# Attention with three probability buffers and a reordered turn; linear attention written out over sixteen blocks

## The chip, the cores and the metric

The kernel runs on one core of one Trainium2 chip. The metric is the device time of one execution in microseconds; of a kernel the median of its runs is taken. Before the change it is 1459.32 us, the median of three runs between 1455.14 and 1463.46 us.

The engines that appear below are PE (TensorE, matrix multiplications; its weight loads are listed as PEld), ACT (ScalarE), DVE (VectorE), POOL (GpSimd) and SP, which issues DMAs.

## The reference

The reference is a small transformer-like network over 16 images of 113 tokens (36 patches and 77 text tokens) with 256 features. Four layers follow each other, each an attention-like block and a feed-forward block with residuals. Only two blocks matter here, cut to their core:

```python
# third layer, its attention part: no softmax
theta_x = einsum('bnf,lf->bnl', x, W_theta)      # 64 latent features
phi_x   = einsum('bnf,lf->bnl', x, W_phi)
fun_g_x = einsum('bnf,of->bno', x, W_g)
att     = einsum('bnl,bml->bnm', theta_x, phi_x) / 16
out     = einsum('bnm,bmo->bno', att, fun_g_x)

# fourth layer, its attention part: 16 heads of 16 features
Wqk     = einsum('hij,hkj->hik', tril, tril)
scores  = einsum('bshe,bthe->bhst', x_h @ Wqk, x_h) / 4
attn    = softmax(scores)
out     = (attn @ (x @ Wv.T + bv)) @ Wo.T + bo
```

All is in 32-bit floats, and x is the layer-normalised state.

## The kernel before

The state `core.h` stays on chip as 113 rows by 16 blocks (images) by 256 features. Before each block a stage normalises it and turns it to features by tokens, split into two 16-bit halves, `xt_hi` and `xt_lo`. A product of two 32-bit matrices is then three 16-bit matmuls, made by `mm3` (lines 459 to 463): high by high, high by low, low by high. A result that feeds another product is split in the same way: ACT rounds it to the high half, DVE or POOL subtracts to get the low half. Each stage is one program block, in which every engine runs its own written-out or looped order, and engines wait for one another on counting semaphores. `need(eng, sem, n)` is such a wait that is left out for counts of zero or less.

**Linear attention** (`stage_linear_attention`, line 2775). Since no softmax stands between, phi and g are first multiplied to a 64 by 256 matrix per image. Four operations of PE: `theta` for a group of four images (2 x 3 matmuls of 452 columns), `project` for one image (6 matmuls of 320 columns: phi and g side by side), `collect` (phi times g, 3 matmuls of 256 columns), `spread` (theta times that matrix, 3 matmuls). In the profile their results are la_pth, la_ppg, la_pm and la_po, in this order. ACT and DVE split after `theta`, `project` and `collect`; DVE adds the result of `spread` to the state. A hardware loop runs over the four groups; `theta` has one buffer, so a pass starts with `theta`, and the order of a pass is project(0), then for each j: project(j+1), collect(j), spread(j-1), at last spread(3). The other buffers are double.

**Attention** (`stage_attention`, line 3079). Written out over 17 turns; turn j works on image j, ahead on j+1 and j+2, behind on j-1. Per image the 16 heads go in four groups g of four. `project_u` makes the head-wise factors, `take_q` (ACT) and `split_u` (DVE) split them, `first_pass` makes scores for the row maxima, DVE takes the maxima, repeats them (`repeat_peaks`), PE transposes them (`turn_peaks`), ACT and DVE split them (`take_qm`, `split_peaks`), and `second_pass` makes the scores again with the maximum subtracted. Then per group: `exponential` (ACT, line 3309) into a 32-bit buffer `prob`, `round_prob` (ACT, line 3315) into `prob_hi`, POOL's subtraction into `prob_lo` (line 3146), and `weigh_v` on PE (line 3228, 20 small matmuls), which also makes the sums of the rows. `project_v` makes the values, and `normalize`, `take_o`, `split_o`, `project_out`, `add` finish the image. `keep_warm` issues four matmuls whose result nobody reads. `prob` has two buffers: exponential g waits for the low half of g-2.

Beside this, each turn prepares two pieces of the weights of the last stage (`CutWeights`): ACT casts both (line 1515), scales one in place (line 1520), POOL subtracts for the scaled one (line 1530, behind `prob_lo` of its turn), DVE for the other (line 1524). SP loads the pieces.

The order of ACT in a turn before the change: exponential 0 and 1, take_v, round_prob 0 and 1, take_q(j+2), exponential 2 and 3, take_o(j-1), round_prob 2 and 3, take_qm(j+1), two casts, one scaling. PE's: second_pass(0), first_pass(j+1, 0), keep_warm, second_pass(2), project_u(j+2), first_pass(j+1, 2), keep_warm, weigh_v 0 and 1, project_v(j+1), turn_peaks(j+1), project_out(j-1), weigh_v 2 and 3.

Of the kernel before, what the change touches and what calls it, by code (L numbers as in the profile page):

```python
# [6 lines left out]
F16 = mybir.dt.float16  # L7
I32 = mybir.dt.int32
U32 = mybir.dt.uint32
ALU = mybir.AluOpType  # L10
# [3 lines left out]
NB = 16  # L14
# [2760 lines left out]
def stage_linear_attention(nc, core, d, w):  # L2775
# [3 lines left out]
    with Stage(nc, "la") as st:  # L2779
        wt_hi, wt_lo, wg_hi, wg_lo = w.wt_hi, w.wt_lo, w.wg_hi, w.wg_lo  # L2780
        th_hi, th_lo = (st.sb(n, [Z, GT], F16) for n in ("th_hi", "th_lo"))
        two = range(2)
        pg_hi, pg_lo = ([st.sb(f"{n}{p}", [L, W2], F16) for p in two] for n in ("pg_hi", "pg_lo"))
        m_hi, m_lo = ([st.sb(f"{n}{p}", [Z, D], F16) for p in two] for n in ("m_hi", "m_lo"))
        pth = st.ps("pth", [Z, 512])
        ppg, pm, po = ([st.ps(f"{n}{p}", [s, 512]) for p in two] for n, s in (("ppg", L), ("pm", Z), ("po", L)))
        th_ready, th_high, th_split = st.sem("th_ready"), st.sem("th_high"), st.sem("th_split")
        g_ready, g_high, g_split, m_ready, m_high, m_split, o_ready, o_free = (
            [st.sem(f"{n}{p}") for p in two] for n in (
                "g_ready", "g_high", "g_split", "m_ready", "m_high", "m_split", "o_ready", "o_free"))  # L2790
        with nc.Block() as block:
            @block.tensor
            def _(pe):
                with pe.Fori(0, NG) as q:
                    cols = bass.ds(q * GT, GT)
                    pe.wait_ge(th_split, q)
                    for k in range(KC):
                        last = mm3(pe, pth[:, 0:GT], wt_hi[:, k, :], wt_lo[:, k, :], core.xt_hi[:, k, cols],
                                   core.xt_lo[:, k, cols], k == 0, k == KC - 1)
                    last.then_inc(th_ready, 1)  # L2800

                    def project(j):
                        p = j % 2
                        tok = bass.ds(q * GT + j * L, L)

                        pe.wait_ge(g_split[p], q * 2 + j // 2)
                        for k in range(KC):
                            last = mm3(pe, ppg[p][:, 0:W2], core.xt_hi[:, k, tok], core.xt_lo[:, k, tok],
                                       wg_hi[:, k, :], wg_lo[:, k, :], k == 0, k == KC - 1)
                        last.then_inc(g_ready[p], 1)  # L2810

                    def collect(j):
                        p, before = j % 2, q * 2 + j // 2
                        pe.wait_ge(g_split[p], before + 1)
                        pe.wait_ge(m_split[p], before)
                        mm3(pe, pm[p][:, 0:D], pg_hi[p][:, 0:Z], pg_lo[p][:, 0:Z], pg_hi[p][:, Z:W2],
                            pg_lo[p][:, Z:W2], True, True).then_inc(m_ready[p], 1)

                    def spread(j):
                        p, before = j % 2, q * 2 + j // 2  # L2820
                        pe.wait_ge(th_split, q + 1)
                        pe.wait_ge(m_split[p], before + 1)
                        pe.wait_ge(o_free[p], before)
                        tok = slice(j * L, (j + 1) * L)
                        mm3(pe, po[p][:, 0:D], th_hi[:, tok], th_lo[:, tok], m_hi[p][:], m_lo[p][:], True,
                            True).then_inc(o_ready[p], 1)

                    project(0)
                    for j in range(GB):
                        if j + 1 < GB:  # L2830
                            project(j + 1)
                        collect(j)
                        if j:
                            spread(j - 1)
                    spread(GB - 1)

            @block.scalar
            def _(act):
                with act.Fori(0, NG) as q:
                    act.wait_ge(th_ready, q + 1)  # L2840

                    for p in two:
                        act.wait_ge(o_ready[p], q * 2)
                    act.activation(th_hi[:], pth[:, 0:GT], ACT.Copy, scale=1.0 / WS).then_inc(th_high, 1)
                    for j in range(GB):
                        p, before = j % 2, q * 2 + j // 2
                        act.wait_ge(g_ready[p], before + 1)
                        act.wait_ge(m_ready[p], before)
                        act.activation(pg_hi[p][:], ppg[p][:, 0:W2], ACT.Copy, scale=1.0 / WS).then_inc(g_high[p], 1)
                        act.wait_ge(m_ready[p], before + 1)  # L2850
                        act.wait_ge(o_ready[p], before)
                        act.activation(m_hi[p][:], pm[p][:, 0:D], ACT.Copy, scale=1.0 / 16).then_inc(m_high[p], 1)

            @block.vector
            def _(dve):
                def add(q, j):
                    p = j % 2
                    dve.wait_ge(o_ready[p], q * 2 + (j // 2 + 1))
                    b = bass.ds(q * GB + j, 1)
# [3 lines left out]
                with dve.Fori(0, NG) as q:  # L2863
# [3 lines left out]
                    for j in range(GB):  # L2867
# [7 lines left out]
                        if j:  # L2875
                            add(q, j - 1)
# [755 lines left out]
```

## Time and profile before

| | us |
|---|---|
| median of three runs | 1459.32 |
| the profiled execution | 1472.0 |
| its span | 1470.3 |
| PE busy | 1047.1 (71%) |
| DVE busy | 1028.9 (70%) |
| ACT busy | 751.0 (51%) |
| POOL busy | 519.4 (35%) |

The profile is of one execution, not of the median run. Times in rows count from the start of its span. The program is a sequence of stages with different limits, so that the shares above say little about any one; the rows below are of the two stages at hand, at 865 to 918 us and 1062 to 1238 us.

### The profile page before, as it was taken

The page shows a single profiled execution, that of the slowest core. Times are in us where ns is not written, and L with a number is a line of the kernel's source. Part 1 is how long each engine was busy: PE and PEld are TensorE (multiplying, and loading weights), DVE is VectorE, ACT ScalarE, POOL GpSimd, SP SyncE. Part 2 cuts the span into 40 slices and gives each one's busy share as a digit, 9 for nine tenths or more (in the row PEclk, how much of TensorE's full clock was granted, in tenths as well). Part 3 has the DMA queues.
Part 4 walks back from the last instruction along what each step waited for, and adds up shares of the span by engine and source line. Part 5 has one row for each costly group of instructions (what it writes and reads, how often), then busy time and mean ns, then how long its engine had stood idle before and what let it go on. Part 6 is the DMA issues. An engine that isn't in the chain of part 4 may idle for free. (4 is left out here: it accounts for less than half of the span.)

```text
span 1470.3 us, 28385 instructions
## 1 busy us (share of the span) xinstructions
PE 1047.1 (71%) x9099; PEld 705.2 (48%) x9099; DVE 1028.9 (70%) x2229; ACT 751.0 (51%) x1493; POOL 519.4 (35%) x620
## 2 busy tenths in 40 slices
PE   3558877753699986766658867266589995389991
PEld 2322322232356553554446744144466663388880
DVE  5779999987256445567967654788758887646552
ACT  5557777742476653125437632244358885244440
POOL 0249888850444427501011100000136665122204
PEclk9669999975799998788978978589669997589996
DMA  5001111000465644202000000000013331112214
GB/s 227 15 22 37 43 43 43 29 26 26 129 165 149 165 137 135 70 6 86 1 0 1 1 1 0 0 0 0 19 69 107 114 117 57 47 51 66 66 48 122
DMA packets 50687, 89.84 MB, mean 61 GB/s; under 512 B 8555, under 2 KB 34867, under 8 KB 49715
## 3 DMA queue, kind: packets, MB, share of 16 engines
q1 hardware_dynamic: 43360, 67.20, 14.3%
q0 software_dynamic: 6912, 18.88, 4.8%
q10 hardware_dynamic: 288, 2.10, 0.5%
q8 instruction: 76, 1.25, 0.3%
q14 instruction: 51, 0.42, 0.1%
HBM read 72.11 MB, written 16.04 MB: 60 GB/s over the span
## 5 line engine op out<-in xcount | busy, mean ns | idle before, releaser
L1133 POOL TENSOR_TENSOR scan_ch<-scan_hs,scan_ct 128x452 f32<-128x452 f32 x128 | 143.6, 1143 | 40.7 <-DVE scan_hs L1247 36.9
L1158 PE MATMUL scan_py<-scan_ch,ident 128*128 128x452 f32 x256 | 131.0, 601 | 37.7 <-POOL scan_ch L1133 28.0
L1247 DVE TENSOR_TENSOR_SCAN scan_hs<-scan_abar,scan_bx 128x452 f32<-128x452 f32 x128 | 133.2, 1084 | 1.2 <-DVE scan_bx L1239 0.6
L2224 DVE TENSOR_SCALAR m3x_a<-m3x_ph,m3x_b 128x128 f32<-128x128 f32 x184 | 49.7, 343 | 68.4 <-ACT m3x_ah L2202 66.2
L1158 PEld LDWEIGHTS scan_py<-scan_ch,ident 128*128 128x128 f32 x256 | 40.6, 193 | 107.0 <-POOL scan_ch L1133 100.2
L1207 ACT ACTIVATE scan_abar<-ssm_dt,ssm_a 128x448 f32<-128x448 f32 x128 | 79.8, 634 | 13.2 <-DVE scan_hs L1247 12.7
L2202 ACT ACTIVATE m3x_ah<-m3x_ph,m3x_b 128x128 f16<-128x128 f32 x184 | 50.1, 383 | 65.0 <-PE m3x_ph L463 60.9
L3146 POOL TENSOR_TENSOR mha_prob_lo<-mha_prob,mha_prob_hi 113x452 f16<-113x452 f32 x64 | 65.8, 1051 | 38.2 <-ACT mha_prob_hi L3315 38.2
L461 PE MATMUL m3x_ph<-m3x_xb,m_w_hi 128*128 128x128 f16 x368 | 74.3, 223 | 2.6 <-DVE m3x_al L2235 2.2
L462 PE MATMUL m3x_ph<-m3x_xb,m_w_hi 128*128 128x128 f16 x368 | 74.4, 224 | 0.0
L463 PE MATMUL m3x_ph<-m3x_xb,m_w_lo 128*128 128x128 f16 x368 | 74.2, 223 | 0.0
L1239 DVE TENSOR_TENSOR scan_bx<-scan_pb,ssm_dx 128x452 f32<-128x452 f32 x128 | 73.2, 615 | 0.4 <-PE scan_pb L1145 0.4
L2020 DVE TENSOR_TENSOR m0x_a<-m0x_ph,m0x_gate 128x256 f32<-128x256 f32 x57 | 24.2, 424 | 68.1 <-ACT m0x_gate L1980 67.8
L669 POOL TENSOR_SCALAR mhaf_xr<-h,rstd,mhaf_shift 113x256 f32<-113x256 f32 x5 | 2.9, 592 | 193.9 <-DVE mhaf_shift L734 193.9
L2297 POOL DMA_INDIRECT shared_got<-m_out,m_slot x48 | 50.3, 1048 | 48.5 <-issue 34.9
L1889 POOL DMA_INDIRECT m0x_xg<-m_rows,m0x_idx x57 | 57.4, 1007 | 15.7 <-POOL m0x_idx L1887 15.4
L1202 ACT ACTIVATE scan_ct<-scan_pc 128x452 f32<-128x452 f32 x64 | 34.5, 539 | 39.1 <-POOL scan_ch L1133 25.0
L461 PE MATMUL m3x_py<-m_w_hi,m3x_ah 128*128 x184 | 50.1, 272 | 1.0 <-DVE m3x_yo L2242 0.8
L463 PE MATMUL m3x_py<-m_w_hi,m3x_al 128*128 x184 | 50.1, 272 | 0.0
L462 PE MATMUL m3x_py<-m_w_lo,m3x_ah 128*128 x184 | 50.1, 272 | 0.0
L1530 POOL TENSOR_TENSOR m_w_lo<-mha_wbuf,m_w_hi 128x1024 f16<-128x1024 f32 x16 | 34.1, 2130 | 32.9 <-ACT mha_wbuf L1520 32.9
L1921 PE MATMUL m0x_ph<-m_w_hi,m0x_xb 128*128 x114 | 44.3, 389 | 1.1 <-ACT m0x_xb L1973 1.1
(697 smaller groups left out, 3808.2 us busy)
## 6 DMA issues: line engine op xcount, KB each, us to landing
mha_wbuf<-m3w SPq DMA_DIRECT2D x32, 512.0 KB, 3.3
scan_piece<-m0w SPq DMA_DIRECT2D x30, 256.0 KB, 2.7
m0x_b<-m0b SPq DMA_DIRECT2D x57, 128.0 KB
m_out<-m0x_yo SPq DMA_DIRECT2D x57, 128.0 KB
tok_wbuf<-m0w SPq DMA_DIRECT2D x5, 768.0 KB, 9.4
m3x_b<-m3b SPq DMA_DIRECT2D x23, 128.0 KB, 3.1
m_out<-m3x_yo SPq DMA_DIRECT2D x23, 128.0 KB
m_rows<-m0r_parts SPq DMA_DIRECT2D x4, 448.0 KB
```

The source lines that it names most:

```text
L461: pe.matmul(out, w_hi, x_hi, start=start, stop=False)
L462: pe.matmul(out, w_hi, x_lo, start=False, stop=False)
L463: return pe.matmul(out, w_lo, x_hi, start=False, stop=stop)
L1133: pool.tensor_tensor(ch[r][:], hs[r][:], ct[n % 2][:], ALU.mult).then_inc(weighed, 1)
L1158: pe.matmul(py[c][:, 0:GT], core.ident[:], ch[u % R][:], start=n == 0, stop=n == NS - 1).then_inc(summed, 1)
L1207: act.activation(abar[c][:, 0:GT].rearrange("p (b t) -> p b t", t=L)[:, :, 1:L], ssm.dt[:, c, cols].rearrange("p (b t) -> p b t", t=L)[:, ...
L1239: dve.tensor_tensor(bx[u % R][:], pb[n % 2][:, 0:GT], ssm.dx[:, c, cols], ALU.mult).then_inc(drive, 1)
L1247: dve.tensor_tensor_scan(hs[u % R][:], abar[c][:, 0:GT], bx[u % R][:], 0.0, ALU.mult, ALU.add).then_inc(scanned, 1)
L1889: pool.indirect_dma_start(xg[p][:], None, m.rows[:, :], bass.IndirectOffsetOnAxis(ap=idx[p][:, 0:1], axis=0)).then_inc(gathered[p], 16)
L2202: ins = act.activation(a_hi[r][:, f, :], ph[p][:, f, :], ACT.Relu, bias=b1[p][:, 0, f:f + 1])
L2297: pool.indirect_dma_start(self.got[j][k][:], None, m.out[:, :], bass.IndirectOffsetOnAxis(ap=m.slot[:, b, k:k + 1], axis=0)).then_inc(self ...
L3146: pool.tensor_tensor(prob_lo[g][:], prob[g % 2][:], prob_hi[g][:], ALU.subtract).then_inc(p_low, 1)
```

## The change

Linear attention: the hardware loop over groups is replaced by an order written out over all 16 blocks. `theta` gets two buffers on chip and in PSUM. PE's order is project(0), theta(0), project(1), and then for each block b: collect(b); theta of the next group, if b is the second block of its group; spread(b-1); project(b+2). ACT and DVE follow the same order. The semaphores that were one for each of two buffers become one counter each.

Attention: `prob` has three buffers, so exponential g waits for the low half of g-3. Exponential 2 stands ahead of take_q(j+2). weigh_v(3) of a turn is issued in the next turn, behind second_pass(0) and first_pass(0). The reciprocal of the sums is written into `o` and multiplied in place; the buffer `rec` goes, and the wait for `split_o` of the block before stands ahead of the reciprocal.

```diff
+                project(0)
+                theta(0)
+                project(1)
+                for b in range(NB):
+                    collect(b)
+                    if b % GB == 1 and b // GB + 1 < NG:
+                        theta(b // GB + 1)
+                    if b:
+                        spread(b - 1)
+                    if b + 2 < NB:
+                        project(b + 2)
+                spread(NB - 1)
...
+                high_gate(0)
+                high_theta(0)
+                high_gate(1)
+                for b in range(NB):
+                    high_memory(b)
+                    if b % GB == 1 and b // GB + 1 < NG:
+                        high_theta(b // GB + 1)
+                    if b + 2 < NB:
+                        high_gate(b + 2)
...
+                for b in range(NB):
+                    low_memory(b)
+                    if b % GB == 1 and b // GB + 1 < NG:
+                        low_theta(b // GB + 1)
+                    if b:
+                        add(b - 1)
+                    if b + 2 < NB:
+                        low_gate(b + 2)
+                add(NB - 1)
...
-        prob = [st.sb(f"prob{r}", [L, HG, L]) for r in two]
+        prob = [st.sb(f"prob{r}", [L, HG, L]) for r in range(3)]
...
-                        pool.tensor_tensor(prob_lo[g][:], prob[g % 2][:], prob_hi[g][:],
+                        pool.tensor_tensor(prob_lo[g][:], prob[(j * 4 + g) % 3][:], prob_hi[g][:],
...
                     if ahead1:
                         first_pass(j + 1, 1 - p, 0)
+                    if behind:
+                        weigh_v(j - 1, 1 - p, 3)
                     if now:
                         keep_warm(4)
                         second_pass(j, p, 2)
...
                     if now:
                         weigh_v(j, p, 2)
-                        weigh_v(j, p, 3)
...
-                    need(act, p_low, j * 4 + (g - 1))
-                    act.activation(prob[g % 2][:], heads(s2[g % 2]), ACT.Exp, scale=0.25).then_inc(exped, 1)
+                    need(act, p_low, j * 4 + (g - 2))
+                    act.activation(prob[(j * 4 + g) % 3][:], heads(s2[g % 2]), ACT.Exp, scale=0.25).then_inc(exped, 1)
...
+                    if now:
+                        exponential(j, 2)
                     if ahead2:
                         take_q(j + 2)
                     if now:
-                        exponential(j, 2)
                         exponential(j, 3)
...
-                    need(dve, o_made, j)
-                    dve.reciprocal(rec[:], pacc[:, KC * L:2 * KC * L]).then_inc(rec_ready, 1)
+
+                    need(dve, ol_ready, j)
+                    dve.reciprocal(o[:], pacc[:, KC * L:2 * KC * L]).then_inc(rec_ready, 1)
                     dve.wait_ge(rec_ready, j + 1)
-
-                    need(dve, ol_ready, j)
-                    dve.tensor_tensor(o[:], pacc[:, 0:KC * L], rec[:], ALU.mult).then_inc(o_made, 1)
+                    dve.tensor_tensor(o[:], pacc[:, 0:KC * L], o[:], ALU.mult).then_inc(o_made, 1)
```

## Rows read from the trace of the kernel before

**Rows 1.** Table by stretches: busy time by engine (instructions), granted clock, DMA.

```profile
core 0: us, PE busy (x) PEld busy (x) DVE busy (x) ACT busy (x) POOL busy (x), PEclk, DMA share, GB/s
865.60:918.20 52.60, 42.35 (x216) 25.61 (x216) 21.65 (x52) 13.82 (x36) 0.00 (x0) 0.86 0.00 0
870.00:879.00 9.00, 6.38 (x41) 3.76 (x39) 4.34 (x11) 2.65 (x8) 0.00 (x0) 1.00 0.01 2
879.00:883.00 4.00, 4.00 (x15) 2.52 (x16) 1.05 (x2) 0.86 (x2) 0.00 (x0) 0.58 0.00 0
...
1108.50:1222.20 113.70, 105.02 (x2358) 75.93 (x2356) 96.67 (x167) 99.39 (x179) 74.29 (x60) 1.00 0.35 114
```

**Rows 2.** Timeline of PE, linear attention: start, duration, instruction, idle time before.

```profile
899.59 0.30 PE L461 MATMUL la_pm<-la_pg_hi 113*64 113x256 f16 x1 [0.36 <-DVE la_pg_lo L2870]
900.03 0.32 PE L461 MATMUL la_po<-la_m_hi,la_th_hi 64*113 64x256 f16 x1
900.50 0.34 PE L461 MATMUL la_ppg<-la_wg_hi,xt_hi 128*113 128x320 f16 x1
...
903.91 0.30 PE L461 MATMUL la_pm<-la_pg_hi 113*64 113x256 f16 x1 [1.19 <-DVE la_pg_lo L2870]
...
905.97 0.37 PE L461 MATMUL la_pth<-xt_hi,la_wt_hi 128*64 x1
...
907.23 0.34 PE L461 MATMUL la_ppg<-la_wg_hi,xt_hi 128*113 128x320 f16 x1
...
908.09 0.30 PE L461 MATMUL la_ppg<-la_wg_hi,xt_hi 128*113 128x320 f16 x1
...
909.30 0.30 PE L461 MATMUL la_pm<-la_pg_hi 113*64 113x256 f16 x1 [0.24 <-DVE la_pg_lo L2870]
```

**Rows 3.** Timeline of DVE, linear attention.

```profile
900.55 0.42 DVE L2873 SCALAR_TENSOR_TENSOR la_m_lo<-la_pm,la_m_hi 64x256 f16<-64x256 f32 x1 [1.02 <-ACT la_m_hi L2852]
```

**Rows 4.** Timeline of ACT, one attention turn.

```profile
1146.39 1.06 ACT L1520 ACTIVATE mha_wbuf<-mha_wbuf 128x1024 f32<-128x1024 f32 x1
...
1150.05 0.64 ACT L3290 ACTIVATE mha_q<-mha_pu,mha_to_q 128x452 f16<-128x452 f32 x1 [0.52 <-PE mha_pu L463]
...
1151.77 0.55 ACT L3309 ACTIVATE mha_prob<-mha_s 113x452 f32<-113x452 f32 x1 [0.46 <-POOL mha_prob_lo L3146]
...
1153.59 0.36 ACT L3303 ACTIVATE mha_qm<-mha_pt,mha_to_qm 128x113 f16<-128x113 f32 x1
...
1155.87 1.06 ACT L1520 ACTIVATE mha_wbuf<-mha_wbuf 128x1024 f32<-128x1024 f32 x1
```

**Rows 5.** Timeline of POOL, the same turn.

```profile
1147.53 2.13 POOL L1530 TENSOR_TENSOR m_w_lo<-mha_wbuf,m_w_hi 128x1024 f16<-128x1024 f32 x1 [1.82 <-ACT mha_wbuf L1520]
1149.62 2.05 POOL L3146 TENSOR_TENSOR mha_prob_lo<-mha_prob,mha_prob_hi 113x452 f16<-113x452 f32 x2
```

**Rows 6.** Timeline of PE, the same turn.

```profile
1148.47 0.26 PE L3203 MATMUL mha_s<-mha_same 32*113 32x113 f16 x2 [0.32 <-ACT mha_prob L3309]
...
1151.72 0.23 PE L3228 MATMUL mha_pacc<-mha_prob_hi,mha_v_hi 113*32 113x113 f16 x4
...
1153.24 0.32 PE L3190 MATMUL mha_pt<-ident,mha_peaks 113*128 113x113 f32 x1
...
1155.24 0.23 PE L3228 MATMUL mha_pacc<-mha_prob_hi,mha_v_hi 113*32 113x113 f16 x4 [0.32 <-POOL mha_prob_lo L3146]
```

**Rows 7.** Timelines of ACT and DVE, the first turns and the last.

```profile
1087.59 1.06 ACT L1520 ACTIVATE mha_wbuf<-mha_wbuf 128x1024 f32<-128x1024 f32 x1
1099.02 1.06 ACT L1520 ACTIVATE mha_wbuf<-mha_wbuf 128x1024 f32<-128x1024 f32 x1
1222.21 1.06 ACT L1520 ACTIVATE mha_wbuf<-mha_wbuf 128x1024 f32<-128x1024 f32 x1
1226.56 0.55 ACT L3309 ACTIVATE mha_prob<-mha_s 113x452 f32<-113x452 f32 x1 [1.22 <-POOL mha_prob_lo L3146]
...
1231.99 1.56 DVE L3395 RECIPROCAL mha_rec<-mha_pacc 128x226 f32<-128x226 f32 x1
```

More of the change, by code:

```diff
@@ L2793, in _, with theta @@
             def _(pe):
-                with pe.Fori(0, NG) as q:
-                    cols = bass.ds(q * GT, GT)
-                    pe.wait_ge(th_split, q)
+                def theta(q):
+                    p, cols = q % 2, slice(q * GT, (q + 1) * GT)
+                    need(pe, th_split, q - 1)
                     for k in range(KC):
-                        last = mm3(pe, pth[:, 0:GT], wt_hi[:, k, :], wt_lo[:, k, :], core.xt_hi[:, k, cols],
+                        last = mm3(pe, pth[p][:, 0:GT], wt_hi[:, k, :], wt_lo[:, k, :], core.xt_hi[:, k, cols],
@@ L2812, in collect @@
[L2812 to L2835, printed above, removed]
+                def project(b):
+                    p, tok = b % 2, slice(b * L, (b + 1) * L)
+                    need(pe, g_split, b - 1)
+                    for k in range(KC):
+                        last = mm3(pe, ppg[p][:, 0:W2], core.xt_hi[:, k, tok], core.xt_lo[:, k, tok],
+                                   wg_hi[:, k, :], wg_lo[:, k, :], k == 0, k == KC - 1)
+                    last.then_inc(g_ready, 1)
@@ new lines, in collect, with spread @@
+                def collect(b):
+                    p = b % 2
+                    pe.wait_ge(g_split, b + 1)
+                    need(pe, m_split, b - 1)
+                    mm3(pe, pm[p][:, 0:D], pg_hi[p][:, 0:Z], pg_lo[p][:, 0:Z], pg_hi[p][:, Z:W2],
+                        pg_lo[p][:, Z:W2], True, True).then_inc(m_ready, 1)
+                def spread(b):
+                    p, g = b % 2, b // GB % 2
+                    pe.wait_ge(th_split, b // GB + 1)
+                    pe.wait_ge(m_split, b + 1)
+                    need(pe, o_free, b - 1)
+                    tok = slice(b % GB * L, (b % GB + 1) * L)
+                    mm3(pe, po[p][:, 0:D], th_hi[g][:, tok], th_lo[g][:, tok], m_hi[p][:], m_lo[p][:], True,
+                        True).then_inc(o_ready, 1)
@@ L2840, in _ @@
                     act.wait_ge(th_ready, q + 1)
[L2842 to L2852, printed above, removed]
+                    need(act, o_ready, (q - 1) * GB)
@@ L2863, in _, with low_theta, low_gate @@
[L2863 removed]
+                def low_theta(q):
+                    p = q % 2
                     dve.wait_ge(th_high, q + 1)
[L2865 removed]
+                    dve.scalar_tensor_tensor(th_lo[p][:], pth[p][:, 0:GT], 1.0 / WS, th_hi[p][:], ALU.mult,
                                              ALU.subtract).then_inc(th_split, 1)
[L2867 to L2877 removed]
+                def low_gate(b):
+                    p = b % 2
+                    dve.wait_ge(g_high, b + 1)
+                    dve.scalar_tensor_tensor(pg_lo[p][:], ppg[p][:, 0:W2], 1.0 / WS, pg_hi[p][:], ALU.mult,
+                                             ALU.subtract).then_inc(g_split, 1)
```

65 lines of the change are left out of this document (32 added, 33 removed).

## The prediction

> **What bounds the kernel now.** I read the page first: no engine is busy for more than 71% of the span, so an average decides nothing, and the two stages that the change touches have to be read by themselves. Next came the table by stretches. Linear attention runs from 865.6 to 918.2 us with the matmul engine (PE) busy 42.35 of 52.6 us at a mean granted clock of 0.86; the clock is 1.00 (2.4 GHz) at 870 to 879 us, but 0.58 at 879 to 883, where for most of the time the lower level, 1.2 GHz, was granted [rows 1]. The attention turns run at 1.00 [rows 1]. The timelines by engine followed.
>
> Linear attention has two kinds of lost PE time. Within a group of four blocks PE waits on each round trip through ScalarE (ACT) and VectorE (DVE): a `collect` waits up to 1.19 us for `pg_lo` [rows 2]. At the seams between loop passes PE drains and restarts with `theta`; 879 to 883 is such a seam.
>
> Attention is paced differently. One turn (one image) lasts 9.48 us: the scaling of the weight buffer, ACT's last work in a turn, starts at 1146.39 and again at 1155.87 [rows 4]. Inside the turn ACT idles 0.52 us before `take_q` (for PE) and 0.46 us before the fourth exponential (for GpSimd, POOL) [rows 4]. These two are what the change removes from ACT. But whether they set the turn must be read from a closed loop of dependencies, and there is one whose links all touch: ACT scales the buffer (1146.39), POOL subtracts `m_w_lo` from 1147.53 for 2.13 us, then, back to back, `prob_lo` 0 and 1 from 1149.62 for 2.05 us, until 1151.67 [rows 5]; PE's `weigh_v(1)` starts at 1151.72; after it and `project_v`, the transpose of the peaks starts at 1153.24 and lasts 0.32, until 1153.56 [rows 6]; ACT's `take_qm` starts at 1153.59, and behind it, after the two casts of the weights, the next scaling at 1155.87 [rows 4]. The steps are 1.14 + 2.09 + 2.10 + 1.52 + 0.35 + 2.28 = 9.48 us: the whole turn, with no slack in it.
>
> **The change, part by part.**
>
> *Three probability buffers.* The fourth exponential then waits for `prob_lo` 0 (half way through the pair, about 1150.65) in place of `prob_lo` 1 (1151.67): 0.46 us of ACT per turn is gone. *Third exponential ahead of `take_q`.* It runs in the 0.52 us in which ACT waited for PE's `pu`: its scores come from the second pass that PE started at 1148.47 [rows 6], before the projection that `take_q` waits for. Together 0.98 us of ACT per turn. What is late next? `take_qm`. It stands behind `round_prob` 3, which now ends about 1 us earlier, but its input still comes at 1153.56, by the loop above, and no link of that loop is touched: same subtraction, same `prob_lo` 0 and 1, same PE order from `weigh_v(1)` to the transpose, same casts. So ACT trades two short waits for one of about 1 us before `take_qm`, and the turn stays 9.48. Value for the 13 turns from 1099.02 to 1222.21 (their scalings start 14 times in that stretch, 9.48 apart on the mean: 123.19 / 13 [rows 7]): 0 us. The bounds: no loss below 0, and the most it could give is B below.
>
> *`weigh_v(3)` moved behind the next turn's first two passes.* Before, it waited 0.32 us for `prob_lo` 3 and started at 1155.24 [rows 6], at the end of the turn. Its 20 matmuls of 113 columns, four side by side, take some 0.3 to 0.4 us (estimate: at 0.86 us for six matmuls of 320 columns [rows 2], five steps of 113 make 0.25, and the change of operation is on top). Now PE goes straight to the second pass, which fills the scores some 0.7 us earlier; ACT cannot use them earlier, being still at its scaling until about 1156.9. The 20 matmuls then lie ahead of four warming matmuls and of the second pass of groups 2 and 3, which waited 0.32 us for ACT's exponential, until 1148.47 [rows 6]. They bring no more work to PE before that point than was taken away ahead of the first passes, so it is reached no later than before. Queued behind it on PE is everything from those warming matmuls on; on DVE `normalize` waits for it, but stands behind two maxima and `split_v`; on ACT `take_v` waits for it, about 1 us later. Cost: 0 in the turns at full clock. In turn 1, which lasts 11.43 us [rows 7] and which I read as paced by PE at half clock, I allow 0.1 us.
>
> *Reciprocal written into `o`.* It waits for `split_o` of the block before, which DVE itself issued earlier in its order: 0, and no instruction is added.
>
> *The last turn and the tail.* Turn 15 has no `take_q` and no `take_qm`, so the loop is open there. Its third exponential waited 1.22 us for `prob_lo` 0 and started at 1226.56 [rows 7], the fourth one subtraction (1.03) later. Now only the fourth waits for `prob_lo` 0, and starts where the third did: 1.0 us earlier. Everything behind it (`take_o`, two roundings, casts, DVE's `low`, and the last `normalize`, at 1231.99 [rows 7]) moves up by some 1.0. Attention in sum: 0 - 1.0 + 0.1 = -0.9 us.
>
> *Linear attention written out.* The work is the same (16 blocks, 4 `theta`); what changes is that the order runs across groups with double-buffered `theta` and `project` two blocks ahead. At full clock, start to start: collect to spread 0.44, spread to project 0.47, a whole project 0.86 (907.23 to 908.09), theta 1.26 (905.97 to 907.23) [rows 2]. Sum on PE: 16 x (0.44 + 0.47 + 0.86) + 4 x 1.26 = 28.3 + 5.0 = 33.3 us.
> Do the round trips fit in? `spread(b)` needs `m_lo`: collect at 899.59, `m_lo` from 900.55 for 0.42 [rows 2, 3], 1.4 us; the new order gives it a block and a collect, 1.77 + 0.44 = 2.2. `collect` needs `pg_lo`: 907.23 to 909.30 is 2.07 us [rows 2]; the new order gives 0.86 + 1.77 = 2.6. DVE has three operations a block like the one of rows 3 (0.42 us for 256 columns; some 1.3 us, an estimate), ACT two, against 1.77 us. So PE runs without a gap in the middle, and I take it that it keeps full clock there. To the 33.3 come: the start at half clock (1.9 us: I take it for as long as at the seam of rows 1, 3.8 us, and half of it lost), the last three blocks, where no project lies between (2.07 - 1.77 = 0.3, and 1.4 - 0.44 - 0.47 = 0.5), and the last result's way through DVE after PE's own time (0.8, about one latency and one 0.42): 36.8 us in place of 52.6. Gain 15.7 us.
> Bounds: if a block went on taking 2.16 us, half of the way from the collect at 899.59 to the one at 903.91 [rows 2], 16 x 2.16 + 5.0 + 3.5 = 43 us, a gain of 9.5; if the start cost nothing extra and the tail were hidden, 34.5 us, a gain of 18.
>
> A rule that speaks against this: the Trainium skill, "TensorE: Matmul & The Clock Gate", section "A second HAM failure mode: psum-queue depth-cycling", says that a kernel which cycles through PSUM banks in each iteration idles PE in tiny gaps often enough that its clock swings between both levels. The new order does cycle through eight banks. By that rule the stage would keep its drops; in this trace the drops stand at the seams, where PE waits on the round trip before and after, and the attention turns, which also go round several banks, hold 1.00 [rows 1]. I give it a share of rival C.
>
> **Sum.** 15.7 + 0.9 = 16.6 us. The profiled execution took 1472.0 us (span 1470.3 and 1.7 around it), so 1455.4 by its own time. It was 0.87% slower than the median of the runs, 1459.32; scaled, 1455.4 x 1459.32 / 1472.0 = 1443 us.
>
> **The rivals.**
> A (forecast): as above, 1443.
> B: the turn follows ACT's own work. Then each of the 13 turns shrinks from 9.48 to what PE needs, 9.48 less its waits of 0.32 and 0.32 [rows 6] and some 0.1 at `weigh_v(1)`: 8.74, 9.6 us more: 1433. (ACT alone would allow 8.50.) For it: ACT is the engine with the most work in a turn and both its gaps go. Against: the closed loop of rows 4 to 6, which would have to be wrong in a link; I looked for slack in each and found at most 0.1 us. The Trainium skill, "Perfetto Trace Analysis", section "Optimization Strategy", reads a gap that repeats on the busy engine as too few buffers. By it the third buffer alone would give 0.46 us in each of 13 turns, 6 us; the 0.46 gap does repeat [rows 4], and I hold that it is not the one that paces.
> C: linear attention keeps part of its loss, by the round trip (2.16 us a block) or by half-clock stretches as at 879 to 883 [rows 1]. Gain 9.5 in place of 15.7: 1449. For it: no such dense order of these operations is in the trace. Against: the slack of 0.8 and 0.5 us in the two round trips above.
> D (other side): PE's clock in attention. The move joins two short waits of PE into one of some 0.7 us a turn, and if the granted clock fell for it, turns would be paced by PE at half clock, as I read turn 1: from the scaling at 1087.59 to that at 1099.02 [rows 7], 11.43 us, 1.95 more than 9.48. Nine such turns of the 13 eat the whole gain; with all 13 it is 25.4 us, 1443 + 25 = 1468, slower than before. Against: PE's idle time per turn does not grow, and the clock held 1.00 with waits of this size spread over the turn.
>
> **How the numbers follow.** A 0.69, B 0.09, C 0.16, D 0.06. About 0.5% (7.3 us) is what a measurement of this kernel can tell from no change, since its three runs spread over 8 us. Faster by more than that means below 1452.0: A, B and nearly all of C, 0.90; within it: the rest of C and the mild cases of D, 0.06; slower: 0.04. The predicted time is A's, 1443. The range is 1435 to 1451: A with its bounds (gain 9.5 to 18 in linear attention) and the spread of the runs, C's 1449 inside, half of B's way inside, B's end and D left out.
>
> **What would show it.** Right: linear attention in 36 to 38 us, PE busy throughout at clock 1.0 but for the first 4 us; attention turns still 9.48 us from scaling to scaling, ACT's waits for `pu` and `prob_lo` gone, a wait of about 1 us before `take_qm` in their place; the end of attention some 16.6 us earlier. Wrong: turns of 9.0 us or less (B), a granted clock below 0.9 in the middle of linear attention or collects that wait for `pg_lo` (C), turns over 10 us (D). A shift of a few us in untouched stages, with no instruction changed, would be the clock falling at other places.

## The result, and the profile after

| | us |
|---|---|
| changed kernel, median of 14 runs | 1451.48 (1448.04 to 1454.98) |
| kernel before, median of 14 runs beside them | 1460.74 (1455.14 to 1463.54) |
| ratio | 0.9939, 95% interval [0.9926, 0.9951] |
| predicted | 1443, range 1435 to 1451 |
| profiled execution of the changed kernel, its span | 1449.0, 1447.3 |

Faster by 9 us where 16 were forecast. The two profiled executions are 23 us apart, of which 13 lie ahead of linear attention (865.6 against 852.9 us at its start), where no instruction differs; they belong to no part of the change. So each stage is compared by its own length.

*Linear attention* did what was forecast. The old order starts with `theta`, the new one with project(0), 1.75 us ahead of its first `theta`. From PE's first instruction of the stage (852.86) to the end of DVE's last addition (890.56) it lasts 37.7 us, against 52.5 in the profile before and 51.8 in a second profile of the old order (run e2 below). The table by stretches, which begins at the first `theta`, answers to [rows 1]:

```profile
core 0: us, PE busy (x) PEld busy (x) DVE busy (x) ACT busy (x) POOL busy (x), PEclk, DMA share, GB/s
854.60:890.60 36.00, 34.87 (x211) 22.01 (x210) 20.96 (x52) 15.19 (x36) 0.00 (x0) 0.97 0.00 1
858.00:888.00 30.00, 29.98 (x190) 19.55 (x189) 18.26 (x47) 13.83 (x33) 0.00 (x0) 1.00 0.00 1
```

PE is busy 29.98 of 30 us at full clock; no seam is left. The timeline of PE answers to [rows 2]: the start, from collect to collect 1.86 us, and a stall of the tail.

```profile
852.86 0.49 PE L461 MATMUL la_ppg<-la_wg_hi,xt_hi 128*113 128x320 f16 x1 [1.91 <-PEq L663]
...
862.37 0.30 PE L461 MATMUL la_pm<-la_pg_hi 113*64 113x256 f16 x1
...
864.23 0.30 PE L461 MATMUL la_pm<-la_pg_hi 113*64 113x256 f16 x1
...
889.60 0.29 PE L461 MATMUL la_po<-la_m_hi,la_th_hi 64*113 64x256 f16 x1 [0.50 <-issue]
```

*Attention* did not. It should have become 0.9 us shorter and became 4.8 us longer: from the first write of `pu` to the last of `pvo`, 174.3 us before and 179.1 after. By turns 1 to 15 (scaling to scaling): 11.43, thirteen of 9.46 to 9.48 and 9.05 before; 11.54, eight of 9.47 or 9.48, then 9.54, 9.65, 9.66, **14.99**, 9.47 and 8.32 after. A normal turn on ACT answers to [rows 4]:

```profile
1141.14 1.04 ACT L3349 ACTIVATE mha_prob_hi<-mha_prob 113x452 f16<-113x452 f32 x2
1143.25 0.36 ACT L3337 ACTIVATE mha_qm<-mha_pt,mha_to_qm 128x113 f16<-128x113 f32 x1 [1.07 <-PE mha_pt L3223]
...
1145.53 1.06 ACT L1520 ACTIVATE mha_wbuf<-mha_wbuf 128x1024 f32<-128x1024 f32 x1
```

Both short waits are gone and one of 1.07 us ahead of `take_qm` stands in their place. But the roundings `prob_hi` 2 and 3, directly ahead of it, moved too. In [rows 4] they must have ended by 1153.59, when `take_qm` started without a wait; now they end 1.07 us ahead of it. POOL's `prob_lo` 2 and 3, which follow them, move with them onto other work of DVE. DVE's and POOL's timelines of two turns, a normal one and the first slow one (`x2` is two instructions in one line):

```profile
1141.72 0.23 DVE L3418 TENSOR_SCALAR mha_peaks<-mha_peak 113x128 f32<-113x128 f32 x1
1141.86 1.24 DVE L3438 TENSOR_TENSOR mha_ot_lo<-mha_o,mha_ot_hi 128x226 f16<-128x226 f32 x1
...
1151.30 1.09 DVE L3418 TENSOR_SCALAR mha_peaks<-mha_peak 113x128 f32<-113x128 f32 x1
1152.31 1.25 DVE L3438 TENSOR_TENSOR mha_ot_lo<-mha_o,mha_ot_hi 128x226 f16<-128x226 f32 x1
```

```profile
1141.79 2.21 POOL L3179 TENSOR_TENSOR mha_prob_lo<-mha_prob,mha_prob_hi 113x452 f16<-113x452 f32 x2 [0.46 <-ACT mha_prob_hi L3349]
...
1151.26 2.04 POOL L3179 TENSOR_TENSOR mha_prob_lo<-mha_prob,mha_prob_hi 113x452 f16<-113x452 f32 x2 [0.46 <-ACT mha_prob_hi L3349]
```

In the kernel before, POOL's pair began at 1153.14 in the turn of [rows 4], behind both operations of DVE, and the groups of instructions of DVE give their means over 15 and 14 turns:

```profile
L3404 DVE TENSOR_TENSOR mha_ot_lo<-mha_o,mha_ot_hi 128x226 f16<-128x226 f32 x15 | 5.9, 395 | 5.8 <-ACT mha_ot_hi L3320 5.8
L3383 DVE TENSOR_SCALAR mha_peaks<-mha_peak 113x128 f32<-113x128 f32 x14 | 3.2, 227 | 0.5
```

Now `split_o` (the line of `ot_lo`) lasts 1.24 us in every turn, and `repeat_peaks` 0.23 where it starts 0.07 us ahead of POOL's pair, but 1.09 where it starts 0.04 behind. That is on the loop, since the transpose waits for it. What puts it behind is a slip of 0.09 us in the tenth turn. DVE's reciprocal starts 0.34 us behind the start of `v_lo` in turn 9 and 0.43 in turn 10, and the maxima and `repeat_peaks` follow it:

```profile
1138.28 0.42 DVE L3405 SCALAR_TENSOR_TENSOR mha_v_lo<-mha_pvo,mha_v_hi 113x256 f16<-113x256 f32 x1
1138.62 1.56 DVE L3431 RECIPROCAL mha_o<-mha_pacc 128x226 f32<-128x226 f32 x1
...
1147.76 0.42 DVE L3405 SCALAR_TENSOR_TENSOR mha_v_lo<-mha_pvo,mha_v_hi 113x256 f16<-113x256 f32 x1
1148.19 1.57 DVE L3431 RECIPROCAL mha_o<-mha_pacc 128x226 f32<-128x226 f32 x1
```

With both stretched DVE is full (19.00 of 19.20 us), PE waits 0.85 us for `ot_lo`, the turn lasts 9.65, and after three turns with a stretched `repeat_peaks` PE's clock falls to the lower level, which makes one turn of 14.99:

```profile
1145.50:1164.70 19.20, 16.91 (x370) 11.94 (x366) 19.00 (x28) 16.44 (x30) 12.47 (x10) 1.00 0.35 113
1164.70:1174.40 9.70, 8.85 (x209) 6.38 (x197) 9.63 (x15) 8.24 (x16) 6.29 (x5) 1.00 0.33 110
1174.40:1189.40 15.00, 15.00 (x223) 10.99 (x216) 9.88 (x16) 8.45 (x16) 6.32 (x5) 0.54 0.22 72
```

```profile
1153.61 0.32 PE L461 MATMUL mha_pvo<-mha_wo_hi,mha_ot_hi 128*113 128x256 f16 x1 [0.85 <-DVE mha_ot_lo L3438]
...
1163.26 0.32 PE L461 MATMUL mha_pvo<-mha_wo_hi,mha_ot_hi 128*113 128x256 f16 x1 [0.85 <-DVE mha_ot_lo L3438]
...
1172.91 0.32 PE L461 MATMUL mha_pvo<-mha_wo_hi,mha_ot_hi 128*113 128x256 f16 x1 [0.84 <-DVE mha_ot_lo L3438]
```

### The profile page after: what moved, and what is told of

Same layout as the page of the kernel before. It is cut to its first block and busy times, and to the rows that moved or that the text cites. A ratio compares the mean times of both kernels' runs of the same rounds, so it can differ in the third digit from the quotient of the medians.

```text
span 1447.3 us, 28190 instructions
## 1 busy us (share of the span) xinstructions
PE 1039.5 (72%) x9099; PEld 702.8 (49%) x9099; DVE 1040.7 (72%) x2229; ACT 750.4 (52%) x1493; POOL 521.0 (36%) x620
## 5 line engine op out<-in xcount | busy, mean ns | idle before, releaser
L1889 POOL DMA_INDIRECT m0x_xg<-m_rows,m0x_idx x57 | 57.6, 1010 | 15.7 <-POOL m0x_idx L1887 15.7
```

The lines of the kernel that those rows point to most:

```text
L1889: pool.indirect_dma_start(xg[p][:], None, m.rows[:, :], bass.IndirectOffsetOnAxis(ap=idx[p][:, 0:1], axis=0)).then_inc(gathered[p], 16)
```

## Experiments

All in one table; "attention" and the turns are of each kernel's one profile, medians and ratios of four to six timed executions (twelve for e2) beside the kernel before (1459 to 1461 us). "Full turns" are turns 2 to 14, "others" their lengths: where one value stands, nearly all have it. "clock" marks turns that the clock's fall made long.

| run | median us | ratio [95%] | attention | turn 1 | others |
|---|---|---|---|---|---|
| e1 linear part only | 1443.67 | 0.9878 [0.9859, 0.9896] | 171.9 | 9.47 | 9.47 |
| e2 attention part only | 1461.68 | 1.0012 [0.9995, 1.0028] | 174.5 | 13.05 | 9.48 |
| e3 roundings held | 1446.98 | 0.9899 [0.9881, 0.9918] | 175.4 | 13.03 | 9.48, one 9.55 |
| e4 weigh_v(3) back | 1447.46 | 0.9907 [0.9888, 0.9925] | 176.3 | 9.48 | 9.48, 9.56, clock 13.96 |
| e5 peaks first | 1439.65 | 0.9869 [0.9846, 0.9892] | 168.2 | 8.59 | 8.85 or 9.74 |
| e7 fill | 1443.95 | 0.9901 [0.9881, 0.9921] | 174.8 | 13.01 | 9.48, 9.55, 9.58 |
| e10 weigh_v(3) moved only | 1445.70 | 0.9912 [0.9893, 0.9931] | 175.7 | 13.05 | 9.47 |
| e11 held, weigh_v(3) back | 1443.23 | 0.9902 [0.988, 0.9923] | 172.0 | 9.48 | 9.49, one 9.55 |
| e13 values early | 1443.34 | 0.9867 [0.9829, 0.9906] | 171.8 | 11.65 | clock 13.53, 12.6; 8.66 |
| e14 low behind peaks | 1445.15 | 0.9900 [0.9872, 0.9928] | 175.7 | 12.57 | 9.47 |
| e15 e14 and e5 | 1430.45 | 0.9805 [0.9775, 0.9835] | 161.2 | 8.58 | 8.85 |
| e16 e15, weigh_v(3) back | 1435.09 | 0.9834 [0.9804, 0.9863] | 164.5 | 8.58 | 9.10 |
| e17 e10 and warm end | 1443.02 | 0.9889 [0.9867, 0.9911] | 172.7 | 9.48 | 9.48 |
| e18 e14 and warm end | 1440.48 | 0.9874 [0.9851, 0.9897] | 171.4 | 9.47 | 9.48 |
| e19 changed again | 1451.72 | one execution | 181.9 | 13.05 | 9.48, 9.55, clock 14.01, 10.75 |

**The halves of the change.** e1 is the kernel before with the new `stage_linear_attention`, e2 the changed kernel with the old one.

> Attention as before, linear attention as changed. T1 (linear attention gives some 15.7 us, and the changed attention takes about 5 back, because POOL's prob_lo 2 and 3 now run beside DVE's repeat_peaks and split_o and stretch them from 0.23 to 1.1 and from 0.40 to 1.24 us, so that DVE paces some turns and PE's clock falls): 15 to 17 us under the kernel before, attention from its first take_q to its last add 174 us as before. T3 (linear attention gives only some 9 us in the median, and what the profile of the changed kernel shows in attention is chance): 8 to 10 us under it.

> Linear attention as before, attention as changed. T1: 3 to 7 us slower than the kernel before, split_o at 1.24 us in most turns, some turns of 9.65 us or more. T2 (what costs is the new place of weigh_v(3) on PE, not DVE): the same time. T3: 1 us faster, at most equal.

The linear half alone is worth 1.22%, 17.8 us by the ratio, all of the change's gain and more; the attention half alone gives nothing (0.9995 to 1.0028), and on top of the linear half it costs 7.8 us (1451.48 less 1443.67). In e2 `split_o` is 1.24 us in the full turns, `repeat_peaks` 0.23, and no turn behind turn 1 is long: the stretch of `split_o` alone costs no time. Its profile also suggests why the halves do not add up: it has no slip in turn 10, and the kernel before, to which it is compared, has the long turn 1 already (11.43), which e1 has not (9.47).

**Taking the stretch away.** e3 holds ACT's roundings 2 and 3 back until DVE has written `ot_lo`; e14 leaves ACT alone and holds POOL.

```diff
 e3, ACT:
+                        need(act, ol_ready, j)
                         round_prob(j, 2)
 e14, POOL:
                         pool.wait_ge(p_high, j * 4 + (g + 1))
+                        if g == 2 and j + 1 < NB:
+                            pool.wait_ge(peaks_ready, j + 2)
```

> The changed kernel with one more wait on ACT: round_prob 2 of a turn waits until split_o of the block before is done, so that POOL starts prob_lo 2 behind it. T1: repeat_peaks back at 0.23 and split_o at 0.40 us, every full turn 9.48, no fall of the clock, 5 to 7 us under the changed kernel (about 1445). T2: DVE's durations fall too, but the time stays at the changed kernel's 1451.

> The changed kernel, but GpSimd begins prob_lo 2 only after VectorE has written the repeated peaks of the next block. Theory of the stretch (the extra time of attention comes from GpSimd's subtraction falling on VectorE's repeat_peaks, 0.23 to 1.1 us, which makes a turn of 9.65 and then a fall of the clock): repeat_peaks 0.23 in all turns, split_o still 1.24, all full turns 9.48, no turn of 14 to 15, attention 174 to 176 us (turn 1 stays at 13.0), total 1444 to 1447. Theory that the turns grow and the clock falls for another reason: a turn of 9.6 or more, or one over 13 behind turn 1, is still there, total about 1451.

In both every `repeat_peaks` is 0.23 and every `split_o` 0.39 in the full turns (in e14 I had expected 1.24: the wait delays POOL by just enough to let it by), and no turn behind turn 1 is over 9.55. DVE's groups in e18, which has e14's wait:

```profile
L3443 DVE TENSOR_TENSOR mha_ot_lo<-mha_o,mha_ot_hi 128x226 f16<-128x226 f32 x15 | 5.8, 389 | 0.9 <-ACT mha_ot_hi L3359 0.9
L3423 DVE TENSOR_SCALAR mha_peaks<-mha_peak 113x128 f32<-113x128 f32 x14 | 3.2, 227 | 0.5
```

The changed kernel has 1238 and 507 there. The medians are 4.5 (e3) and 6.3 us (e14) under the changed kernel's; e3's interval lies clear of it, e14's just touches it. Turn 1 stayed long in both: another cause. In e14 the clock did not come up there at all: it is 0.50 from 1031.9 to 1069.4.

**The place of weigh_v(3).** e4 is the changed kernel with `weigh_v(3)` back at the end of its own turn; e10 is e1 with only that move; e11 is e3 and e4 together.

```diff
 e4, PE (e10 the other way round):
-                    if behind:
-                        weigh_v(j - 1, 1 - p, 3)
...
                         weigh_v(j, p, 2)
+                        weigh_v(j, p, 3)
```

> The changed kernel with weigh_v(3) back at the end of its own turn. T1: DVE's two operations stay stretched, DVE can still pace; the time stays within 2 us of the changed kernel's 1451, or above it. T2: 5 to 7 us under the changed kernel, about 1445, turns of 9.48.

> Linear attention as changed, attention as before but for weigh_v(3), which is issued in the next turn as in the changed kernel. If the three runs add up (1443.7 without any change of attention, 1447.0 with the moved weigh_v and the hold on ACT, 1447.5 with the rest of the change and weigh_v at its old place): 1446 to 1448, and the loss in turn 1 (13.0 us in place of 9.5 or 11.4), at half clock. If the move costs nothing by itself: 1443 to 1445.

> The changed kernel with both: weigh_v(3) back at the end of its turn, and round_prob 2 held until split_o is done. Nothing is stretched on DVE and PE's order is the one before. If the two causes (stretch on DVE, weigh_v moved) are all of it: 1443 to 1445, like the kernel with linear attention alone, every full turn 9.48. If the third buffer and the moved exponential have a cost of their own: 1446 or more.

With `weigh_v(3)` moved and the rest of PE's order as it was, turn 1 is 11.54 to 13.05 us in seven profiles (changed kernel twice, e2, e3, e7, e10, e14), at its old place 9.47 or 9.48 in three (e1, e4, e11) and 11.43 in the kernel before. So the fall also comes with the work in place; in the kernel before the clock came up 22.4 us behind the first write of `pu`, in e1 21.6. And in e5 and e15 below, where `weigh_v(3)` is moved too but PE transposes the peaks earlier, turn 1 is 8.59 and 8.58, without a fall. e11, with both causes out, has attention at 172.0, e1's value. Three pairs differ in this alone: 175.7 against 171.9 (e10, e1), 175.4 against 172.0 (e3, e11), and the changed kernel's 179.1 and 181.9 against 176.3 (e4). The ratios of single pairs overlap, so the size rests on the profiles. e4 itself fits neither of its forecasts: 4 us under the changed kernel, with the fall behind a stretched `repeat_peaks` still in it.

The 2 us windows ahead of the fall, e1 first, then e10, both 22 us behind the first write of `pu`:

```profile
1055.10:1057.10 2.00, 1.79 (x58) 1.17 (x57) 0.73 (x2) 1.12 (x2) 0.01 (x1) 1.00 0.00 0
1057.10:1059.10 2.00, 1.65 (x40) 1.18 (x35) 2.00 (x4) 1.97 (x3) 0.00 (x0) 1.00 0.04 8
1059.10:1061.10 2.00, 1.00 (x26) 0.74 (x25) 1.61 (x4) 2.00 (x6) 1.71 (x1) 1.00 0.52 104
```

```profile
1057.30:1059.30 2.00, 1.54 (x38) 0.93 (x37) 0.73 (x2) 1.13 (x2) 0.05 (x1) 1.00 0.00 0
1059.30:1061.30 2.00, 1.65 (x48) 1.42 (x46) 2.00 (x4) 1.97 (x3) 0.00 (x0) 0.73 0.04 8
1061.30:1063.30 2.00, 2.00 (x30) 0.87 (x20) 1.64 (x4) 2.00 (x6) 1.72 (x1) 0.50 0.41 96
```

In both the clock has risen 0.4 to 0.5 us before the first row; in e10 PE has 0.25 us less to do, the 20 matmuls that left, waits 0.46 us for `am` where e1 waits 0.21, and the clock goes back to 0.50 for some 10 us.

**Is it the missing work or the order?** e17 is e10, e18 is e14, each with two unread matmuls where `weigh_v(3)` stood. e7 is the changed kernel with four such matmuls ahead of `project_out`, where PE waits for a stretched `split_o`.

```diff
 e17, e18 (e7: range(4), ahead of project_out):
                         weigh_v(j, p, 2)
+                        need(pe, exped, j * 4 + 4)
+                        for _ in range(2):
+                            pe.matmul(s2[0][:, 0:384], core.xt_hi[:, 0, 0:L], core.xt_hi[:, 1, 0:384], start=True, stop=True)
```

> The changed kernel with four more matmuls of 384 columns, whose result nobody reads, ahead of project_out, where PE waits up to 0.85 us for split_o once repeat_peaks and split_o are both stretched. If the fall of PE's clock in attention comes from that wait: no turn of 13 us or more at full length, DVE's stretch and turns of 9.65 us remain, time 1446 to 1449. If the fall has another cause (the wait ahead of the second pass): it is seen as often, 1451. If PE is short of time in a turn: slower than 1453.

> Old attention with weigh_v(3) moved, as in the run with the move alone (turn 1 13.05 us, attention 175.7), plus two unread matmuls of 384 columns where weigh_v(3) stood at the end of the turn: they leave the rest of the output untouched. Theory of the missing work (moving weigh_v(3) leaves the matrix engine less busy around the rise of the clock in turn 1 and the clock falls again): with the place filled, turn 1 is about 9.5 us, attention 172, total 1442 to 1445. Rival (what matters is that weigh_v(3) stands between the passes and delays what follows it, or turn 1 goes by chance): turn 1 stays at 13, total 1445 to 1448.

> The changed kernel with both causes answered and its order kept: GpSimd's prob_lo 2 waits for the repeated peaks, and two unread matmuls stand where weigh_v(3) was. If the two causes are all that attention lost: turn 1 about 9.5, all other full turns 9.48, attention 171 to 172.5, total 1440 to 1443. If turn 1 stays at 12.5 to 13: 1444 to 1447. If a third cause is left: more.

e17's turn 1 is 9.48 with the move in place, and so is e18's (9.47), where e10 had 13.05 and e14 12.57: it is PE's missing work that matters, not the order, as far as one profile of each can tell; the timed medians are 2.7 and 4.7 us lower, with intervals that overlap. e17's windows at the same place hold the full clock:

```profile
1055.20:1057.20 2.00, 2.00 (x40) 1.12 (x39) 0.75 (x2) 1.14 (x2) 0.01 (x1) 1.00 0.00 0
1057.20:1059.20 2.00, 1.65 (x58) 1.30 (x53) 2.00 (x4) 1.97 (x3) 0.00 (x0) 1.00 0.03 8
```

e7 has a stretched `repeat_peaks` (1.10 us) in a turn of 9.58 and no fall of the clock behind it: filled, PE's wait for `ot_lo` did not lead to one. Its time, 1443.95, is below the 1446 to 1449 that this theory gave. e18 has nothing left: attention 171.4, 0.5 below e1; the last turn, 8.33 in place of 9.05, is the gain that the tail was to give, and the rest of the attention part gives none.

**Once more.** The changed kernel again, one execution.

> The changed kernel once more, one profile. If the stretch of VectorE's operations sets the fall of the clock: split_o near 1.24 in all turns, repeat_peaks near 1.1 in at least one turn, turns of 9.6 there, and a turn of 13 to 15 within two turns after. If the fall of the first profile was chance unconnected with it: stretched turns with no fall, or a fall with no stretched turn ahead. Turn 1 above 11 by the moved weigh_v(3).

The fall came again, one turn after a stretched `repeat_peaks` (9.55, then 14.01), and in e4 too (9.56, then 13.96). In the three profiles with the changed kernel's loop and no fill a `repeat_peaks` stretched in a full turn was followed by it; in e5, whose turns are shorter and where 9.74 comes beside 8.85, it was not. This profile has a second fall, at 0.50 from 1194.9 to 1208.5, which makes turn 14 10.75 us. No stretched `repeat_peaks` stands in the two turns ahead of it; its cause is open.

**Is the closed loop the bound?** e5 shortens it by one edit: the transpose of the peaks goes ahead of `project_v`. e15 adds e14's wait, e16 also puts `weigh_v(3)` back. e13, another way: `project_v` ahead of `weigh_v(0)` in place of four warming matmuls, `repeat_peaks` on ACT, `weigh_v(3)` back.

```diff
 e5, e15, e16, PE:
-                        project_v(j + 1)
                         turn_peaks(j + 1)
+                        project_v(j + 1)
 e13, PE (weigh_v(3) back as in e4):
+                    if ahead1:
+                        project_v(j + 1)
                     if now:
-                        keep_warm(4)
                         weigh_v(j, p, 0)
                         weigh_v(j, p, 1)
                     if ahead1:
-                        project_v(j + 1)
                         turn_peaks(j + 1)
 e13, ACT:
                         round_prob(j, 2)
+                    if ahead1:
+                        repeat_peaks(j + 1, 1 - p)
+                    if now:
                         round_prob(j, 3)
```

> The changed kernel with PE transposing the peaks (turn_peaks) ahead of project_v, so that the closed loop scaling, m_w_lo, prob_lo 0 and 1, weigh_v(1), project_v, transpose, take_qm loses the 0.9 us of project_v, down to where the peaks are ready. Loop theory: full turns fall below 9.48, but DVE with its stretched operations then paces (9.04 us of it with split_o alone stretched, up to 9.65 with repeat_peaks too), so turns of 9.1 to 9.65 and a time of 1445 to 1453. Rival (another loop paces, or ACT or PE by its own work): full turns stay exactly 9.48.

> Matrix engine transposes the next block's peaks ahead of project_v, and GpSimd's prob_lo 2 waits for the repeated peaks. The first alone gave turns of 8.85 us where repeat_peaks took 0.23 and of 9.74 where GpSimd's subtraction fell on it (8 turns of 13), total 1439.7. Theory of the stretch: all full turns 8.85, no repeat_peaks over 0.3, attention 161 to 164 us, total 1432 to 1435. If the wait itself delays GpSimd so that its subtraction becomes the bound, or the clock falls as the matrix engine is fuller: turns of 9.3 or more, total 1439 or above.

> As the run before, with weigh_v(3) at its old place at the end of the turn. Theory of the place of weigh_v(3) (moved, it costs 2 to 3.5 us in turn 1 by the clock's second fall and nothing in the full turns): here turn 1 is not above 9.5 and the full turns are as in the run before, so total equal or lower by up to 3 us: 1430 to 1435. Rival: in shorter turns the move is needed, since exponentials now wait for the second pass behind weigh_v(3): full turns longer by 0.3 or more, total 1437 or above.

> weigh_v(3) at its old place; project_v stands in the place of one set of warming matmuls ahead of weigh_v(0), the peaks are transposed after weigh_v(1), and ScalarE, not VectorE, writes the repeated peaks, between the roundings 2 and 3, so that no VectorE operation can be stretched ahead of take_qm. Closed loop: 9.48 less project_v's share between weigh_v(1) and the transpose (0.9 us) gives 8.6, and ScalarE's own work of 8.5 plus 0.3 for the moved operation 8.8: turns 8.7 to 8.9, total 1430 to 1435. Rival: project_v in the early place delays weigh_v(0) and (1) or the values come late for VectorE: turns 9.2 or more, total 1438 or above.

e5's turns fall into two kinds, 8.85 with `repeat_peaks` at 0.23 and 9.74 with 1.11. Its total, 1439.65, is below the 1445 to 1453 that I expected. e15 removes the second kind: its turns are the 8.85 of the forecast within 0.01 us, its total lies somewhat below it (1430.45 for 1432 to 1435). It beats both kernels: 0.9805 [0.9775, 0.9835] of the one before. Its turn on ACT and POOL:

```profile
1138.04 1.05 ACT L3351 ACTIVATE mha_prob_hi<-mha_prob 113x452 f16<-113x452 f32 x2
1139.33 0.36 ACT L3339 ACTIVATE mha_qm<-mha_pt,mha_to_qm 128x113 f16<-128x113 f32 x1 [0.25 <-PE mha_pt L3225]
1141.61 1.06 ACT L1520 ACTIVATE mha_wbuf<-mha_wbuf 128x1024 f32<-128x1024 f32 x1
```

```profile
1139.07 2.06 POOL L3181 TENSOR_TENSOR mha_prob_lo<-mha_prob,mha_prob_hi 113x452 f16<-113x452 f32 x2 [0.87 <-DVE mha_peaks L3420]
```

In e16 the turn is 9.10: my theory (the move gives nothing in full turns) missed. Its rival was right in kind, but named 0.3 us or more a turn and 1437 or above, and 0.25 and 1435.09 were measured. In the shorter turn the move is worth 0.25 us; by the rival's account because the second pass is late behind `weigh_v(3)`, which I did not follow in the rows. e13 reaches 8.66 us a turn, the shortest, but its first three turns lie at the lower clock wholly or in part, and its time, 1443.34, missed the 1430 to 1435 expected. Its runs lie between 1431 and 1445, and the two fastest have the highest mean clock (0.852 and 0.847, the others 0.837 to 0.840).

## Why the prediction was wrong, step by step

- *What bounds:* right. The loop of six steps paces at 9.48 us, in the changed kernel as before; the one edit that shortens it (e5, e15) gives 8.85.
- *Three buffers and the exponential: "ACT trades two short waits for one of about 1 us before `take_qm`":* right, 1.07 us, turn 9.48. **Here the first step failed.** I followed what is late next and not what is early next: I wrote that `round_prob` 3 "now ends about 1 us earlier", did not ask what that triggers, and set the bound "no loss below 0" without a reason. It starts POOL's `prob_lo` 2 and 3 beside DVE. That made `split_o` 3 times as long in each turn, harmless by itself, and `repeat_peaks`, on which the transpose of my loop waits, 5 times as long whenever it began behind POOL. Cost in the profile: the four turns of 9.54 to 14.99 hold 43.84 us, 5.9 more than four of 9.48. Taken away in e14, the time falls by 6.3 us.
- *weigh_v(3) moved, "0 in the turns at full clock", "in turn 1 ... 0.1 us":* the second failed step. The 0 of the full turns holds (e10: 9.47). Turn 1 I had read as paced by PE at half clock in any case; e1 shows that it can be 9.47. The move costs 2.1 us there in the changed kernel's profile (11.54 against 9.48), 3.6 in e10, e3 and the second profile. Its price is not in the instructions moved but in the fall of the clock, with 0.25 us less for PE to do just behind the rise.
- *Tail, 1.0 us:* right in kind, 0.7 (the last turn 8.32 against 9.05).
- *Together* in attention: 2.1 + 5.9 - 0.7 = 7.3 us more than e1's 171.9, which gives the 179.1 of the profile within 0.1. Forecast -0.9. The kernel before had a fall in turn 1 in its own profile, which is most of why its 174.3 is not the 171.9 of e1 and why the difference of the two profiles shows 4.8 only.
- *Linear attention, gain 15.7, in 36.8 us:* the mechanism right, the size somewhat high. It measured 37.7, a gain of 14.8 against the profile before and 14.1 against e2's. The block took 1.86 for 1.77, which is 1.4 us in sixteen; the start and the tail took 0.5 less than allowed.
- What the forecast did not have: with the new linear attention the unchanged attention of e1 is shorter too, 171.9 for 174.3, as the fall in turn 1 is missing. The two together are 17.2 us, and e1's timed gain is 17.8 (15.2 to 20.6). Whether the kernel before has that fall in most executions was not measured.
- *The rule on cycling through PSUM banks* (the Trainium skill, "TensorE: Matmul & The Clock Gate", section "A second HAM failure mode: psum-queue depth-cycling"), given a share of C: the stage goes round eight banks and held 1.00 for 30 us. The measurement decides against it here.
- *Rival B*, the wait ahead of the fourth exponential as pacing: refuted, the gap is gone and the turn is 9.48. The third buffer buys nothing at this length of the loop.
- *Rival D*, given 0.06: its kind came, a fall of the clock in attention, but in two turns and not in nine or more. In the full turns PE's joined wait (0.55 us) did no harm; they hold 1.00. In turn 1 D was closer than I gave it: the moved `weigh_v(3)` left PE a longer wait, 0.46 for 0.21 us, and the clock fell.
- Forecast 1443, measured 1451.5. With e18's two repairs of attention the same change takes 1440.5.

## What to carry to other kernels

When a wait goes away, ask what starts earlier, on every engine down the line, and what it will lie beside: here an unneeded head start of 1 us put GpSimd onto VectorE's shortest link. One wait that holds the head start back (e14) was worth 6 us, and with the loop shortened as well (e15) 21. Work that looks free to move at full clock may be what holds the clock in the one turn where it has just risen; look at that turn by itself. First find the closed loop, then shorten a link of it; here an edit off the loop, the move of `weigh_v(3)`, paid only afterwards (e16). And measure two orders from the first instruction of each: the new one may not begin with the same operation.

## What the runs showed of the hardware

VectorE operations on SBUF alone are held up by a GpSimd subtraction running beside them: `repeat_peaks`, one input, takes 0.23 us alone and 1.09 to 1.12 where it begins just behind the subtraction, `ot_lo`, two inputs, 0.40 and 1.24. VectorE waits out the whole instruction of the other; they do not share the rate. Two of the changed kernel's stretched `repeat_peaks`, each with the single subtraction under which it began:

```profile
1151.26 1.04 POOL L3179 TENSOR_TENSOR mha_prob_lo<-mha_prob,mha_prob_hi 113x452 f16<-113x452 f32 x1 [0.46 <-ACT mha_prob_hi L3349]
...
1183.13 1.05 POOL L3179 TENSOR_TENSOR mha_prob_lo<-mha_prob,mha_prob_hi 113x452 f16<-113x452 f32 x1 [2.81 <-ACT mha_prob_hi L3349]
```

```profile
1151.30 1.09 DVE L3418 TENSOR_SCALAR mha_peaks<-mha_peak 113x128 f32<-113x128 f32 x1
...
1183.39 0.87 DVE L3418 TENSOR_SCALAR mha_peaks<-mha_peak 113x128 f32<-113x128 f32 x1
```

The first begins 0.04 us behind GpSimd and lasts 1.09, the second 0.26 behind and lasts 0.87; both end 0.08 us after the subtraction has ended. All 33 stretched `repeat_peaks` of the seventeen traces do so, wherever in the subtraction they began (0.005 to 0.54 us behind its start, durations 1.12 down to 0.58), and the 0.08 is the same to 0.003 us. Four that began 0.001 to 0.004 us behind it, three of them in e5, were not stretched. Which comes first decides: 0.07 us ahead cost nothing, 0.04 us behind cost 0.86. GpSimd loses little: its pair takes 2.04 to 2.21, against 2.05 in the kernel before. The Trainium skill, "Perfetto Trace Analysis", section "Optimizing Scalar/DVE Operations", says that GpSimd and VectorE share an SBUF read port and that a VectorE operation with two ports holds it as an exclusive lock. The traces agree that it is exclusive, and show GpSimd holding it against VectorE. That it is this port which holds VectorE up here is read from that page; no run separates it from another cause.

TensorE's clock went back to 1.2 GHz right after rising to 2.4 (e10), for 10 us, where the engine had 1.54 and 1.65 of two stretches of 2 us to do, and stayed up with 1.79 and 1.65 (e1) and with 2.00 and 1.65 (e17). In the kernel before it went back as well, with the work of `weigh_v(3)` in place (1.00 from 1084.4 to 1087.9, 0.50 to 1094.7). No more than these cases is shown.

Open: why VectorE's reciprocal starts 0.09 us late in turn 10. It is the same turn in the changed kernel, e3, e4, e7, e14, e18 and e19, where the reciprocal starts 2.67 us behind the scaling in place of 2.58, and in e11 (2.67 for 2.62), also where nothing is stretched; the turn is 0.06 to 0.08 us longer in all but e14 and e18. The kernel before has it in turn 11, where it costs nothing, and e1, e2, e10 and e17 do not have it. Nothing that it waits for comes later in the trace. It is this slip that brings `repeat_peaks` behind GpSimd in the changed kernel's full turns. And how often each kernel's clock falls over many executions: each has one profile, the changed kernel two.
